# FFN 0 of a four-layer Flamingo block: norm moved into attention layer 0, shared expert directly behind it, routing beside it

## The reference

```python
x = x + tanh(g_xattn[0]) * _L0_xattn_ref(_layernorm(x), ctx, ctx, ...)
x = x + tanh(g_ffn[0])   * _L0_ffn_ref(_layernorm(x), gate_w, W1, b1, W2, b2, sW1, sb1, sW2, sb2)
```

## Time and profile before

| what | us |
|---|---|
| median of 3 runs (1206.77 to 1207.47) | 1206.85 |
| the profiled execution's own time | 1203.48 |
| its span in the trace | 1201.7 |
| TensorE busy | 1013.5 (84%) |
| VectorE busy | 786.7 (65%) |
| ScalarE busy | 630.0 (52%) |
| GpSimd busy | 619.9 (52%) |

### The profile page before, as it was taken

One profiled execution on the slowest core, in us unless ns is written; L12 is line 12 of the kernel. 1 busy time (PEld: TensorE's weight loads), 2 busy tenths in 40 slices (PEclk: granted clock), 3 DMA queues, 4 the chain that ended last, 5 costly groups with the idle time before them and its releaser, 6 DMA issues.

```text
span 1201.7 us, 25230 instructions
## 1 busy us (share of the span) xinstructions
PE 1013.5 (84%) x8940; PEld 818.6 (68%) x8940; DVE 786.7 (65%) x1683; ACT 630.0 (52%) x1447; POOL 619.9 (52%) x650
## 2 busy tenths in 40 slices
PE   1599999863899799996877898999999999856994
PEld 0377676652576799985656666777777777646994
DVE  2889999735301855684699887845555556945674
ACT  1444444332222466665766677765556656634663
POOL 0154545410777600734887776744554446663763
PEclk9899999965799999999899999999999999978997
DMA  7960000000121122421100000000013000002334
GB/s 234 309 178 2 1 1 1 1 1 0 40 66 46 51 72 69 124 72 42 28 19 10 2 1 2 1 2 1 2 50 109 2 1 1 2 32 63 88 109 132
DMA packets 79733, 59.12 MB, mean 49 GB/s; under 512 B 13667, under 2 KB 72419, under 8 KB 79428
## 3 DMA queue, kind: packets, MB, share of 16 engines
q1 hardware_dynamic: 73028, 44.03, 12.9%
q0 software_dynamic: 6592, 13.58, 3.6%
HBM read 35.76 MB, written 25.07 MB: 51 GB/s over the span
## 4 chain that ended last, share of the span: by engine, by line
PE 62%; DVE 17%; issue 9%; ACT 5%; POOL 4%; SPq 2%; DVEq 1%; DMA 1%; ACTq 0%; POOLq 0%
PE psS L1104 8%; PE psT L1624 5%; PE psO L1688 5%; PE psO L1114 5%; PE psS L1680 5%; PE psO L1639 3%; PE psS L1613 3%; PE psO L1043 3%; PE psS L1114 3%; PE psS L1035 3%; DVE rden L750 2%; DVE ring L738 2%; PE psT L616 2%; DVE mx L734 2%; PE psO L1646 2%
## 5 line engine op out<-in xcount | busy, mean ns | idle before, releaser
L1993 POOL TENSOR_TENSOR ring<-ring,mx 128x1024 f32<-128x1024 f32 x96 | 182.1, 1904 | 121.0 <-DVE mx L1874 120.3
L1769 ACT ACTIVATE pT<-psT 128x512 f32<-128x512 f32 x192 | 114.5, 596 | 145.1 <-PE psT L1624 144.9
L1157 ACT ACTIVATE pT<-psS,b1copy 128x128 f32<-128x128 f32 x496 | 141.4, 368 | 89.1 <-PE psS L1104 89.0
L1104 PE MATMUL psS<-ring 128*128 128x128 f32 x992 | 134.1, 279 | 16.1 <-issue 8.7
L1624 PE MATMUL psT<-ident,ring 128*128 128x128 f32 x768 | 124.6, 286 | 12.7 <-ACT pT L1769 7.2
L812 POOL TENSOR_TENSOR ring<-ring,rden 128x1024 f32<-128x1024 f32 x32 | 75.3, 2354 | 116.1 <-DVE rden L752 116.1
L1104 PEld LDWEIGHTS psS<-ring 128*128 128x128 f32 x992 | 122.5, 194 | 18.5 <-issue 11.8
L1866 DVE TENSOR_TENSOR ring<-psS,bias 128x1024 f32<-128x1024 f32 x96 | 112.9, 1217 | 33.6 <-PE psS L1613 33.1
L1624 PEld LDWEIGHTS psT<-ident,ring 128*128 128x128 f32 x768 | 87.6, 144 | 54.2 <-issue 35.2
L1296 POOL DMA_INDIRECT xrows<-sorted_y,rows x64 | 61.9, 967 | 99.3 <-DMA sorted_y<-pT 66.2
L1874 DVE TENSOR_REDUCE mx<-ring 128x16 f32<-128x1024 f32 x96 | 112.0, 1208 | 0.0
(11 more groups left out here) (281 smaller groups left out, 2286.4 us busy)
## 6 DMA issues: line engine op xcount, KB each, us to landing
w<-w_dram SPq DMA_DIRECT2D x34, 256.0 KB, 5.9
sorted_x<-late SPq DMA_DIRECT2D x20, 256.0 KB, 3.9
ring<-sorted_x SPq DMA_DIRECT2D x20, 256.0 KB, 3.3
sorted_y<-pT SPq DMA_DIRECT2D x18, 256.0 KB, 2.8
sorted_z<-blank_dram SPq DMA_DIRECT2D x2, 1584.0 KB, 9.6
ring<-sorted_z SPq DMA_DIRECT2D x12, 256.0 KB
xrows<-token_y SPq DMA_DIRECT2D x8, 256.0 KB, 4.8
ctxz<-ctxz_dram SPq DMA_DIRECT2D x1, 1056.0 KB, 12.0
```

The source lines that it names most:

```text
L1104: mm = nc.tensor.matmul(psS[:, j % 2, f * P:(f + 1) * P], wcopy[:, j % 4, 0, f, :], xgT[:, s, t * P:(t + 1) * P], start=True, stop=True)
L1157: op = nc.scalar.activation(hs[:, j % 2, f, :], psS[:, j % 2, f * P:(f + 1) * P], func, bias=b1copy[:, j % 4, f:f + 1])
L1769: nc.scalar.activation(pT[:, u % 2, 4 * h:4 * h + 4, :].rearrange("p a q -> p (a q)"), psT[:, :], ACT.Exp).then_inc(s_pT, 1)
L1993: nc.gpsimd.tensor_tensor(rows_, rows_, mx[:, u % 4, 0:NH].rearrange("p h -> p h ()").broadcast_to([P, NH, SK]), ALU.subtract).then_inc(s_ ...
```

## The change

What it does:

1. The norm of FFN 0 goes into attention 0. When the four tiles of a chunk have their statistics, GpSimd makes their inverse deviations (`spread_chunk`: 8 small operations), ScalarE norms the four tiles straight into `xrows` (`normalise_chunk`), TensorE transposes them in a PSUM bank that the attention uses too (`turn_chunk`), and ScalarE copies them out once (`keep_chunk`). Chunks 0 to 6 do this inside units 6 to 32, and chunk 7 behind the layer.
2. The logits of chunks 0 to 5 are made in TensorE's units 28 to 33, those of 6 and 7 inside the shared expert.
3. `sum_rows` adds halves: four `tensor_tensor` additions of 512, 256, 128 and 64 numbers, each waiting for the last, in place of one reduce.
4. The shared expert starts directly behind the layer. `rank_tensor` and `setup_tensor` stand between its chunks. On VectorE its additions to x stand between the steps of the routing.
5. The routing chooses on the raw logits; the two weights come from one exponential of their difference, made later (`gates_vector`, inside the routed experts).
6. The 64 scatters read `xrows` and `rows` directly, without staging.
7. The register loops of attention and shared expert are written out.

```diff
-                nc.vector.tensor_reduce(rd, rows, AXX, ALU.add).then_inc(q.esum.sem, 1)
-                dve.wait_ge(*q.esum(u + 1))
+                src, at, n = sp[:, j, :], 0, NH * SK // 2
+                for k in range(4):
+                    to = rd if n == SK else hsum[:, at:at + n]
+                    nc.vector.tensor_tensor(to, src[:, 0:n], src[:, n:2 * n], ALU.add).then_inc(q.esum.sem, 1)
+                    dve.wait_ge(*q.esum(4 * u + k + 1))
+                    src, at, n = to, at + n, n // 2
...
+        def spread_at(k):
+            return (k - 6) // 4 if k % 4 == 2 and k > 5 else None
+        def normed_at(k):
+            return (k - 7) // 4 if k % 4 == 3 and k > 6 else None
+        def turned_at(k):
+            return (k - 8) // 4 if k % 4 == 0 and k > 7 else None
+        def spread_chunk(pool, c):
+            s = c % 2
+            pool.wait_ge(s_stat, NT + CH * (c + 1))
+            if c > 1:
+                pool.wait_ge(s_nr, c - 1)
+            deviations(pool, rows_, lna[:, s:s + 1], lnd[:, s:s + 1], lnr[:, s:s + 1], lnb[:, s:s + 1], lnh[:, s:s + 1], s_dev)
+        def normalise_chunk(act, c):
+            act.wait_ge(s_dev, c + 1)
+            for t in range(CH):
+                op = nc.scalar.activation(xrows[:, c * CH + t, :], x[:, c * CH + t, :], ACT.Identity, bias=lnb[:, c % 2, t:t + 1], scale=lnr[:, c % 2, t:t + 1])
+            op.then_inc(s_nr, 1)
+        def turn_chunk(pe, c):
+            pe.wait_ge(s_nr, c + 1)
+            if c:
+                pe.wait_ge(s_nk, c)
+            for t in range(CH):
+                mm = nc.tensor.transpose(psT[:, t * P:(t + 1) * P], xrows[:, c * CH + t, :], ident[:])
+            mm.then_inc(s_nt, 1)
+        def keep_chunk(act, c):
+            act.wait_ge(s_nt, c + 1)
+            nc.scalar.activation(xnT[:, c * CT:(c + 1) * CT], psT[:, :], ACT.Copy).then_inc(s_nk, 1)
+        def router_logits(pe, c):
+            pe.wait_ge(s_nk, c + 1)
+            for t in range(c * CH, (c + 1) * CH):
+                mm = nc.tensor.matmul(psM[:, t * E0:(t + 1) * E0], xnT[:, t * P:(t + 1) * P], gw[:, 0, :], start=True, stop=True)
+            mm.then_inc(s_lg[0], 1)
...
@@ att_tensor, unit @@
+                if turned_at(k - 1) is not None:
+                    pe.wait_ge(s_nk, turned_at(k - 1) + 1)
...
+                if turned_at(k) is not None:
+                    pe.wait_ge(*q.pT(min(2 * u + 2, 2 * NT)))
+                    turn_chunk(pe, turned_at(k))
+                if k >= NT - 2 * QT:
+                    router_logits(pe, k - (NT - 2 * QT))
                 if qt == 0 and known(k, 0, NT - 2 * QT):
                     scores(b + 2, s, False)
...
@@ att_scalar, end of unit @@
+                if turned_at(k) is not None:
+                    keep_chunk(act, turned_at(k))
                 if known(k, 0, NT - 3):
                     exp_rows(u + 3, (2 * s + qt + 3) % 4)
+                if normed_at(k) is not None:
+                    normalise_chunk(act, normed_at(k))
...
@@ att_gpsimd, unit, behind scale(u + 2) @@
+                if spread_at(k) is not None:
+                    spread_chunk(pool, spread_at(k))
...
@@ shared_tensor @@
+            up(0)
+            router_logits(pe, NC - 2)
+            up(1)
+            turn_chunk(pe, NC - 1)
+            down(0)
+            router_logits(pe, NC - 1)
+            up(2)
+            down(1)
+            rank_tensor(pe, 0)
+            up(3)
+            down(2)
+            up(4)
+            down(3)
+            setup_tensor(pe)
+            for c in range(5, NC):
+                up(c)
+                down(c - 1)
+            down(NC - 1)
...
@@ shared_scalar, behind the gelus of chunk c, and at the end @@
+                if c == 0:
+                    normalise_chunk(act, NC - 1)
+                    keep_chunk(act, NC - 1)
+            route_scalar(act)
...
@@ route_vector(dve, added), where added(c) is shared_sum(dve, c) @@
+            step(nc.vector.scalar_tensor_tensor(pr, oh1, NEG, pr, ALU.mult, ALU.add))
+            added(0)
+            one_hot(oh2, pr, m2)
+            step(nc.vector.tensor_tensor(cnt, oh1, oh2, ALU.add))
...
@@ moe_gpsimd @@
+            spread_chunk(pool, NC - 1)
+            pool.wait_ge(s_nr, NC)
             pool.wait_ge(s_rt[r], ROWS_AT[r])
...
+            for t in range(NT):
+                for m in range(CHOICES[0]):
+                    at = t * CHOICES[0] + m
+                    nc.gpsimd.indirect_dma_start(sorted_x[t // HT], bass.IndirectOffsetOnAxis(rows[:, at:at + 1], 0), xrows[:, t, :], None).then_inc(s_sc[0][t // HT], 16)
```

More of the change, by code:

```diff
@@ L322, in moe_sync @@
             for h in range(2):
-                for s in range(2):
-                    sp_.wait_ge(s_sc[0][s], (h + 1) * CHOICES[0] * HT // 2 * 16)
+                sp_.wait_ge(s_sc[0][h], CHOICES[0] * HT * 16)
                 for s in range(2):
@@ L524, in ln_scalar, with ln_tensor @@
                 evac(NC - 2 + s, s, False)
-        def ln_tensor(pe, n, router, after_first=None, before_last=None):
+        def ln_tensor(pe, n, after_first=None, before_last=None):
             q = LN[n]
[L529 to L534, removed]
             def chunk(c, s, first):
@@ L544, in chunk @@
                 mm.then_inc(q.xt.sem, 1)
-                if router is not None:
-                    logits(c, s)
             for s in range(2):
@@ L724, in att_scalar @@
             exp_rows(2, 2)
-            units(act, unit, 0)
+            units(unit, 0)
+            keep_chunk(act, NC - 2)
         def att_vector(dve, l):
@@ L781, in att_vector @@
                     sum_rows(v - 1, v - 1, True)
-            units(dve, unit, 2)
+            units(unit, 2)
         def att_gpsimd(pool, l):
@@ L842, in route_vector @@
             pr, oh1, oh2, tmp, cnt = (rt[:, k] for k in range(5))
-            m, sm, m1, m2, idx = (rs[:, k] for k in range(5))
+            sm, m1, m2, idx = (rs[:, k] for k in range(1, 5))
             choices = [oh1, oh2][:CHOICES[r]]
@@ L1061, in shared_scalar @@
+            router_logits(pe, NC - 2)
[15 more added lines that the diff above has]
+            down(NC - 1)
         def shared_scalar(act):
             q, nf = FF[0], F0 // P
-            def chunk(c, s, first):
+            for c in range(NC):
+                s = c % 2
@@ L1065, in chunk @@
                 for f in range(nf):
                     act.wait_ge(*q.dup(c * nf + f + 1))
-                    if f == 0 and not first:
+                    if f == 0 and c > 1:
                         act.wait_ge(*q.dy(c - 1))
                     nc.scalar.activation(hT[:, s, f, :], psS[:, f, :], ACT.Gelu, bias=b1[:, 0, E0, f:f + 1]).then_inc(q.dact.sem, 1)
-            for s in range(2):
-                chunk(s, s, True)
-            with act.Fori(1, NC // 2) as i:
-                for s in range(2):
-                    chunk(i * 2 + s, s, False)
@@ L1247, in moe_vector @@
                 if m <= g < m + NC // 2:
+                    if r == 0 and g == m:
+                        gates_vector(dve)
                     if r:
```

226 lines of the change are left out of this document (82 added, 144 removed).

## The result

The changed kernel took 1158.02 us in the median of 4 runs (1153.11 to 1161.52), the kernel before beside it 1206.81 us (1205.94 to 1207.47). The ratio is 0.9593, interval 0.9554 to 0.9632. The forecast was 1157 us, within a range of 1146 to 1168. The profiled execution took 1159.9 us with a span of 1158.1, so it lies 1.9 us above the median, and 6.1 us above the 1153.8 that the sum gave for it. That the median of the runs meets the forecast within 1.0 us is therefore partly luck: several terms were off, with different signs.

A forecast was written before the change was run, and what follows sets the result against it. Bound: 65 us of dependencies with no engine full, then a TensorE wall in the shared expert. 143.62 - 81.6 - 4.6 - 6.7 - 1.0 = 49.7 us saved from 1203.48 gives 1153.8, plus 3.4 for the median: 1157, range 1146 to 1168.

The forecast's parts named there:

- The stretch of 143.62 us: From TensorE's last projection at 244.26 to the shared expert's end at 387.88: 143.62 us, all rebuilt.
- The shared expert, 81.6 us: Rebuilt stretch: 8 chunks at 9.44 us plus logits, transposes, ranks and setup, 81.6 us, assuming the clock stays up.
- Routing at 34 us, margin 1.4: Beside the shared expert: row numbers 34 us in, first half's sorted rows loaded at 80.2, 1.4 us before its end.
- the scatters bound: Rival at the routed experts' start: slower scatters or late row numbers bring the first group 6 us late, 1163; chance 0.12.
- The tree, -2.6: VectorE's sums in attention: four additions take 1.74 us against the reduce's 1.93, over 14 pairs, -2.6 us.
- GpSimd's deviations, +7.8: In the layer: GpSimd's power holds up VectorE's tree additions by 1.3 us in each of 6 chunks, +7.8; bounds 0 to 15.
- no meeting: Rival in the layer: additions miss the deviations or the wait falls where VectorE rests, 7.8 us unpaid, 1149; chance 0.18.
- ScalarE's norm, nothing: In the layer: the norm delays one copy that has slack, costing nothing; without that cover 0.5 each, 3 us.
- The turn, +1.5: In the layer: transposes of chunks 1 to 5 ahead of the scores cost 0.3 us each, +1.5.
- The end of the layer, +4.6: TensorE's units 28 to 33: logits and transposes add 6.3 us, holes hide 1.7, +4.6; bounds 3 and 6.3.
- Routed experts, +1: First 30 us of routed experts: half 1's scatters beside weight copies cost +1 us; bounds 0 and 5.6.
- Slower: Rival in the dense stretch: TensorE's clock falls to 1.2 GHz, 81.6 us more, 1239; chance 0.03.

The follow-up runs named there:

- experiment 10: The changed kernel with the rows staged again before the scatters, on a slower chip: 1286.12 us.
- Experiment 4: The changed kernel with a 128x512 GpSimd addition ahead of a product where the power was, wrong norm scales: 1175.16 us in one run.
- experiment 1: The changed kernel with the one strided reduce of sum_rows back in place of the four additions: 1165.13 us, ratio 0.9652.
- Experiment 3: The changed kernel with GpSimd's power in the deviations replaced by a multiplication, wrong norm scales: 1152.42 us in one run.
- experiment 5: The changed kernel with ScalarE's norm one unit later, behind the next copies, and transposes two units later, on a slower chip: 1288.87 us, ratio 0.9884.
- 11: The changed kernel with ScalarE's norms one unit later and chunk 5 still one unit later, on a slower chip: 1285.56 us.
- 12: The changed kernel with ScalarE's norms one unit later and transposes two units later, run again on a slower chip: 1289.3 us.
- 6: The changed kernel with all 7 logit groups moved behind the first up matmuls, on a slower chip: 1297.54 us, ratio 0.9967.
- 7: The changed kernel with unused matmuls added in TensorE's last layer units, on a slower chip: 1294.35 us, ratio 0.9944.
- experiment 9: The changed kernel again, unaltered, on a slower chip: 1293.56 us against 1309.42 of the kernel before, ratio 0.9886.

## Why the prediction was right, step by step

**The stretch of 143.62 us goes.** Right. From TensorE's last projection to the end of the shared expert it is now 86.95 us (251.80 to 338.75). This is read from the two traces; how much of it items 1, 4, 5 and 6 of the change give each, no experiment separates.

**The shared expert, 81.6 us.** It took 85.15, 3.6 more. The part that failed is "that the clock stays up": the first up matmuls (5.79 for 3.63) and those at 303 us (4.96 for 3.63, clock 0.53) cost 2.2 and 1.3 us. The chunk period was right. One of the prediction's own signs of being wrong, a low clock behind 245 us, did come, and these 3.5 us are its price.

**Routing at 34 us, margin 1.4.** First scatter at 36.6 us, margin about 2 us because the shared expert is longer too. The steps of 0.42 and 0.46 us on VectorE hold. The rival "the scatters bound" did not come, but it was as near as told: staged, they would use up the margin, by the estimate of experiment 10.

**The tree, -2.6.** Its price was right: 0.18 us a pair alone, 0.15 within the change. The count of 14 pairs was too high: alone it brings the 30th inverse 2.1 us forward (223.38 for 225.48).

**GpSimd's deviations, +7.8.** This step failed. The additions were not held up by the power (0.68 us beside it; the two next lose 0.16), so the rival "no meeting" has nearly the right sum for this term, though the meeting itself takes place. The error was in reading: there two operations of 128x1024 stood against four additions, here one on 128x4. Experiment 4 shows the wide kind holding up the first addition by the 1.0 us of the term, experiment 1 and the timeline that the narrow one doesn't.

**ScalarE's norm, nothing.** Failed as well. The prediction looked for the next copy's slack of 0.31 us, but not at what ScalarE itself stands for: GpSimd's chain of 8 small steps, 1.37 us, in front of 1.65 us of norm. Experiment 3 (-0.46 a norm by a shorter chain) and experiment 5 (-0.65 by the order) show it. The stated price "if that cover is gone", 0.5 each, was about right.

**The turn, +1.5.** Not seen: experiment 5 with all its turns is 0.52 us under the tree alone, with the loops written out as a possible help.

All together the interior grew by 0.91 us over 20 units, where 6.7 for the layer was told.

**The end of the layer, +4.6.** From the 30th inverse to first up it is 253.46 - 223.65 = 29.8 us. Before, it was 18.8 to the end of the layer: +11.0. The other three traces of the same code have 27.3, 27.5 and 31.1, so the term is +8.5 to +12.3. With the norm late it is 24.3 to 26.9 (experiments 5, 11 and 12), +5.5 to +8.1, of which a part is still low clock. So the count of logits and transposes was not far off. The missing 4 to 8 us are the wait behind the norm in unit 28 and the time at the low clock; how they divide is not shown. The layer's two terms came to +11.3, and first up to 244.26 + 11.3 = 255.6: it was 253.46. Here too errors of both signs met: that first up came out near the sum is luck. The changed kernel was also 1.8 us ahead at the 10th unit beyond 0.9 for the tree, which stays unexplained; the same code has its 10th inverse between 103.03 and 104.53 in four traces.

**Routed experts, +1.** From the first matmul to the last down it is 162.8 us, before 159.9: +2.9, within its bounds. The penalties cost less than before: TensorE waits 2.18 + 1.51 = 3.7 us beside them, for 5.6. The first 24 matmuls, at the low clock, take 5.3 us for 3.5. And one wait for the weight copies at 461.69 is 2.31 us where it was 0.77: the last steps of the two weights (item 5 of the change) now stand ahead of VectorE's additions to x there, for which the prediction had no term.

In sum: 2.1 us gained against the forecast up to first up, 3.6 lost in the shared expert and 1.9 in the routed experts make 46.3 saved where 49.7 was told. **Slower**, the clock at 1.2 GHz throughout, did not come. But the clock was off in every stage from unit 28 on, in spells of 3 to 10 us. It may also be the source of the spread of 8.4 us between 4 runs, but that is only argued: their mean clocks are 0.960, 0.957, 0.950 and 0.954 from the fastest to the slowest, and the kernel before spread 1.5 us in 4 runs beside them, and 6.9 in 13 runs of the next set.

## What to carry to other kernels

Before a dependent row of small steps is put beside a full engine, look up which engine in the middle consumes its result and what stands behind that consumer in its list: here a wait of 1.37 us on ScalarE cost 0.65 us a chunk in the interior, where the contention that had been feared cost at most the 0.16 us of two small additions, and one unit's delay took that wait away. Take the price of contention only from a meeting of the same shapes: a 128x512 addition on GpSimd cost VectorE 1.03 us, a power on four numbers of nearly the same duration nothing. And when a stretch of small matmuls leads into a dense one, look at the clock of the dense one's first microseconds in short windows, since a stage's mean of 0.95 hides it: in 10 of 12 traces with the norm in the layer the first 8 up matmuls take 5.1 to 6.2 us, and 3.7 only in experiments 6 and 7. Last, trace the same code more than once before reading a difference of a few microseconds behind such a spell.

## What was not expected of the hardware

The clock fell after a single rest of 1.85 us (TensorE busy 1.15 of 3 us from 223 to 226, clock 0.72 and then 0.50 up to 232). It did not fall there after a rest of 1.60 us in experiments 5 and 12. And it fell at 241 us in experiment 11 with TensorE busy 3.00 of 3 us at small matmuls. The Trainium skill (TensorE: Matmul & The Clock Gate, HAM oscillation — how this bites in real kernels) describes a kernel whose clock falls again at each of its waits for a transfer. The first fall here agrees in that it follows a rest, though a rest of another kind; experiment 11 shows a fall without a rest.

On two of the chips TensorE's issue slows down beside a row of indirect transfers from GpSimd, to one matmul in about 2.4 us (28 from 309 to 376 us in experiment 9). The long waits set in 23 to 26 us after the first of the 64 scatters in the six runs without staging (with staging later) and end 6 to 9 us after the last. They come again, 2 to 18 us in sum, beside the 32 gathers near 500 us. The kernel before takes about 100 us more on these chips, but no trace of it there shows whether for the same reason, and on the one where both ran the change saves 16 us instead of 49. That the transfers are the cause is inferred from the times alone. What resource the two would share is open: the trace shows the wait only as "issue".
